# A decoder layer: scores on 32 rows of the array, all four self banks at once, biases added after the products

## What is computed

```
x = x + attention(layernorm(x))          # 16 heads of 32, rotary embedding, causal mask, biases on q, k, v, o
x = x + cross(layernorm(x), ctx)         # q = qdq(x) @ qdq(wq).T + bq ; k, v = ctx @ wkv.T + bkv
                                         # softmax without mask ; out = qdq(o) @ qdq(wp).T + bp
x = x + experts(layernorm(x))            # router softmax over 64 experts, top 8, at most 128 tokens an expert,
                                         # silu(x @ w_gate) * (x @ w_up) @ w_down, weighted sum
```

## Time and profile before

| | |
|---|---|
| three runs without profile | 1936.24, 1941.37, 1945.35 us, median 1941.37 |
| span of the profiled execution | 1982.1 us |
| PE busy | 1741.5 us (88%), 9128 instructions |
| PE weight loads | 1208.5 us (61%) |
| DVE busy | 1257.8 us (63%) |
| ACT busy | 928.6 us (47%) |
| POOL busy | 547.6 us (28%) |

### The profile page before, as it was taken

One profiled execution on the slowest core, in us unless ns is written; L12 is line 12 of the kernel. 1 busy time (PEld: TensorE's weight loads), 2 busy tenths in 40 slices (PEclk: granted clock), 3 DMA queues, 4 the chain that ended last, 5 costly groups with the idle time before them and its releaser, 6 DMA issues.

```text
span 1982.1 us, 31956 instructions
## 1 busy us (share of the span) xinstructions
PE 1741.5 (88%) x9128; PEld 1208.5 (61%) x9128; DVE 1257.8 (63%) x3136; ACT 928.6 (47%) x2737; POOL 547.6 (28%) x564
## 2 busy tenths in 40 slices
PE   3999999999999999999999999999957778778774
PEld 2676666666666666666666666666634455445453
DVE  7677777777777777777777777777743333333332
ACT  3465544555555445555554455555523333332331
POOL 4023223223332232223322322233222221212122
PEclk8999999999999999999999999999968988988887
DMA  9712121111101000000010000000075999998883
GB/s 355 254 45 95 72 81 73 68 60 57 41 25 38 27 21 21 21 21 21 21 34 24 26 21 21 21 21 21 22 197 157 233 237 224 230 229 219 226 216 43
DMA packets 119232, 190.29 MB, mean 96 GB/s; under 512 B 34373, under 2 KB 51141, under 8 KB 119208
## 3 DMA queue, kind: packets, MB, share of 16 engines
q1 hardware_dynamic: 89512, 154.20, 24.5%
q0 software_dynamic: 29696, 35.80, 9.4%
HBM read 126.61 MB, written 119.96 MB: 124 GB/s over the span
## 4 chain that ended last, share of the span: by engine, by line
PE 54%; DMA 22%; DVE 10%; issue 6%; ACT 5%; another core or an unknown queue 2%; POOL 0%; POOLq 0%; SPq 0%; DVEq 0%; ACTq 0%
PE bank L402 28%; DMA out<-x,slots 20%; PE bank L413 7%; PE bank L422 4%; PE bank L408 3%; PE bank L385 3%; ACT probs L678 3%; PE bank L430 3%; DVE kbd L1000 2%; PE bank L438 2%; DVE small L894 1%; PE bank L565 1%; DVE probs L1060 1%; PE bank L390 1%
## 5 line engine op out<-in xcount | busy, mean ns | idle before, releaser
L1224 POOL DMA_INDIRECT routed<-row,slots x256 | 268.2, 1047 | 284.9 <-DVE chosen_before L929 211.4
L678 ACT ACTIVATE probs<-bank,small 128x128 f32<-128x128 f32 x1024 | 322.3, 422 | 47.9 <-DVE small L894 47.2
L1216 POOL TENSOR_TENSOR small<-small,half 128x1 f32<-128x1 f32 x96 | 53.9, 562 | 628.3 <-DVE small L849 628.3
L894 DVE TENSOR_REDUCE small<-bank 128x4 f32<-128x512 f32 x256 | 171.2, 689 | 65.2 <-PE bank L416 47.1
L1304 POOL DMA_INDIRECT out<-x,slots x64 | 99.3, 1552 | 380.6 <-DVE slots L1176 265.4
L678 ACT ACTIVATION_READ_ACCUMULATOR probs<-bank,small 128x1 f32 x512 | 152.2, 301 | 0.0
L422 PEld LDWEIGHTS bank<-idf,probs 128*128 128x128 f32 x1024 | 119.2, 141 | 51.0 <-issue 28.0
L413 PE MATMUL bank<-kbd,qT 128*128 128x512 f32 x256 | 135.9, 612 | 6.7 <-DVE kbd L1000 6.7
L665 ACT ACTIVATE probsT<-bank 128x512 f32<-128x512 f32 x256 | 137.5, 636 | 6.1 <-PE bank L422 3.1
L422 PE MATMUL bank<-idf,probs 128*128 128x128 f32 x1024 | 138.3, 273 | 2.0 <-DVE probs L1060 1.4
L430 PEld LDWEIGHTS bank<-xv,probsT 128*128 128x128 f32 x1024 | 122.7, 193 | 11.1 <-issue 10.3
(11 more groups left out here) (249 smaller groups left out, 3982.4 us busy)
## 6 DMA issues: line engine op xcount, KB each, us to landing
w_gate_up<-in_w_gate SPq DMA_DIRECT2D x64, 384.0 KB
w_gate_up<-in_w_up SPq DMA_DIRECT2D x64, 384.0 KB
w_down<-in_w_down SPq DMA_DIRECT2D x64, 384.0 KB
routed<-empty_row SPq DMA_DIRECT2D x4, 4616.0 KB, 21.5
x_in<-in_x SPq DMA_DIRECT2D x32, 256.0 KB, 2.8
ctx_sb<-in_ctxT_in SPq DMA_DIRECT2D x32, 256.0 KB, 2.8
x_res<-in_x SPq DMA_DIRECT2D x32, 256.0 KB, 2.7
out<-x SPq DMA_DIRECT2D x32, 256.0 KB, 2.0
```

The lines of the kernel that those rows point to most:

```text
L678: last = act.activation(probs[:, g, j * P:(j + 1) * P], bank[:, b, j * P:(j + 1) * P], ACT.Exp, bias=negmax[:, h:h + 1], **({"accum_out": ...
L894: dve.tensor_reduce(negmax[:, g * GH:(g + 1) * GH], bank[:, b, :].rearrange("p (j k) -> p j k", j=GH), AX_X, ALU.max, negate=True).then_in ...
L1224: pool.indirect_dma_start(routed, bass.IndirectOffsetOnAxis(ap=slots[:, k:k + 1], axis=0), row[:, :], None, bounds_check=SLOTS - 1, oob_is ...
```

## The change

Three things at once.

*Scores on 32 rows.* The block-diagonal tiles go. `kT` and `xkT` hold the keys turned, heads of a group on 32 partitions each, and a head's scores are one product of 32 rows by 128 columns. A bank now holds the four heads that share a row group `j` (heads `j`, `j + 4`, `j + 8`, `j + 12`), and the sixteen products go round the four row groups and banks. So all four banks end together. `weigh`, `weigh_turned` and `average` follow the new order of heads, and the rows of Wo and the bias of v are permuted on the host.

*The four self banks at once.* All self scores are issued behind value products 1, with the four mask products ahead of them. Self scores 0 to 3 no longer stand between turns, value products and the turn of xk.

*No bias products.* The biases of q and k are rotated and turned once, and added in the copies to `qT` and `kT`; that of xk in the copy to `xkT`, now on DVE ahead of `norm_probs` 2; that of xv by POOL on `xv1` after the scatter; those of v and o become one table `att_bias` (an extra output projection before the loop), which POOL adds to `x_res` ahead of the scatter.

```diff
-            def project(b, hi, lo, name, first=0, end=1 + 3 * KT):
+            def project(b, hi, lo, name, first=0, end=3 * KT):
...
-                steps = [(bias_of[:, BIASES.index(name), :], bias_rows[:, :])]
+                steps = []
...
-            def scores(b, g, q, kb, causal_mask, done):
-
-                last = pe.matmul(bank[:, b, :], q[:, g, :], kb[:, g, :, :].rearrange("p j t -> p (j t)"),
-                                 start=True, stop=not causal_mask)
+            def scores(banks, rows_of, q, keys, causal_mask, done):
+
                 if causal_mask:
-                    last = pe.matmul(bank[:, b, :], idb[:, :], mask_add[:, :].unsqueeze(1).to_broadcast([P, GH, P]),
-                                     start=False, stop=True)
-                last.then_inc(done, 1)
+                    for b in banks:
+                        pe.matmul(bank[:, b, :], idb[:, :], mask_add[:, :].unsqueeze(1).to_broadcast([P, GH, P]),
+                                  start=True, stop=False)
+                for i in range(NG):
+                    for b, j in zip(banks, rows_of):
+                        own = slice(j * DH, (j + 1) * DH)
+                        last = pe.matmul(bank[:, b, i * P:(i + 1) * P], q[own, i, :], keys[own, i, :],
+                                         start=not causal_mask, stop=not causal_mask or i == NG - 1)
+                        if i == NG - 1:
+                            last.then_inc(done, 1)
...
-                    for g in range(NG):
-                        scores(CROSS_BANK[g], g, cqT, xkbd, False, p_xs)
+                    scores(CROSS_BANK, range(GH), cqT, xkT, False, p_xs)
                 for g in range(NG):
                     if with_cross:
                         until(pe, a_xexp, nth(prev, 4, g + 1))
                         turn_probs(CROSS_BANK[g], g, p_xpT)
-                    if with_self and g < 2:
-                        if g == 0:
-                            until(pe, d_qT, cur)
-                            until(pe, a_kbd, cur)
-                            until(pe, d_kbd, cur)
-                        scores(SELF_BANK[g], g, qT, kbd, True, p_s)
                 if with_self:
                     until(pe, a_xk, cur)
+                if with_cross:
+                    until(pe, g_xvb, prev)
                 for g in range(NG):
                     if with_cross:
                         until(pe, a_xpT, nth(prev, 4, g + 1))
                         weigh(5 if g < 2 else 7, g, xv1, p_xpv)
-                    if g == 0 and with_self:
-                        scores(0, 2, qT, kbd, True, p_s)
+                    if g == 1 and with_self:
+                        until(pe, d_qT, cur)
+                        until(pe, d_kT, cur)
+                        scores(SELF_BANK, range(GH), qT, kT, True, p_s)
                 if with_self:
                     turn(1, xk_sb, p_xkT)
-                    scores(4, 3, qT, kbd, True, p_s)
                     project(3, cT_hi, cT_lo, "xv").then_inc(p_xv, 1)
...
+                project(4, attT_hi, attT_lo, "o").then_inc(s_wT, 1)
...
-                if with_self:
-                    until(act, p_qkT, nth(cur, 2, 2))
-                    until(act, p_s, nth(prev, 4, 4))
-                    spread_keys(6, kbd, (0, 1)).then_inc(a_kbd, 1)
...
-                        if g == 3:
-                            until(act, p_xkT, cur)
-                            until(act, p_xs, nth(prev, 4, 4))
-                            spread_keys(1, xkbd, range(GH)).then_inc(a_xkbd, 1)
...
-                    until(dve, s_x_res, prev * 16)
+                    until(dve, g_res, prev)
...
-                    dve.tensor_scalar(qT[:, :, :].rearrange("p g t -> p (g t)"), bank[:, 2, :], SCALE, None,
-                                      ALU.mult).then_inc(d_qT, 1)
+                    dve.scalar_tensor_tensor(out=qT[:, :, :].rearrange("p g t -> p (g t)"), in0=bank[:, 2, :],
+                                             scalar=SCALE, in1=q_biasT[:, :], op0=ALU.mult,
+                                             op1=ALU.add).then_inc(d_qT, 1)
...
-                    for j in (2, 3):
-                        last = dve.tensor_copy(kbd[j * DH:(j + 1) * DH, :, j, :],
-                                               bank[j * DH:(j + 1) * DH, 6, :].rearrange("p (g t) -> p g t", g=NG))
-                    last.then_inc(d_kbd, 1)
+                    dve.tensor_tensor(wide_a[:, 0:D], bank[:, 6, :], k_biasT[:, :], ALU.add).then_inc(d_kT, 1)
...
+                if with_self:
+                    until(dve, p_xkT, cur)
+                    dve.tensor_tensor(xkT, bank[:, 1, :].rearrange("p (g t) -> p g t", g=NG),
+                                      xk_bias[:, :].unsqueeze(2).to_broadcast([P, NG, P]), ALU.add).then_inc(d_xkT, 1)
                 if with_self:
                     norm_probs(2, cur)
                     norm_probs(3, cur)
...
+                if with_self:
+                    if not with_cross:
+                        pool.wait_ge(s_wprep, 7)
+                    until(pool, s_x_res, cur * 16)
+                    pool.tensor_tensor(x_res[:, :], x_res[:, :], att_bias[:, :], ALU.add).then_inc(g_res, 1)
                 if with_before:
                     scatter(prev - 1)
+                if with_self:
+                    until(pool, a_xv, cur)
+                    pool.tensor_tensor(xv1[:, :, 0:DH], xv1[:, :, 0:DH],
+                                       xv_bias[:, :].rearrange("p (h d) -> p h d", h=H), ALU.add).then_inc(g_xvb, 1)
...
-            for n, kb in enumerate((kbd, xkbd)):
-                pool.wait_ge(s_wprep, n + 2)
-                pool.memset(kb[:, :, :, :], 0.0).then_inc(s_zeroed, 1)
```

More of the change, by code:

```diff
@@ L141, in layer @@
         qT = sb("qT", [P, NG, P])
-        kbd = sb("kbd", [P, NG, GH, P])
+        wide_a = sb("wide_a", [P, 4 * D])
+        kT = wide_a[:, 0:D].rearrange("p (g t) -> p g t", g=NG)
         v_sb = sb("v_sb", [P, D])
@@ L153, in layer @@
         xk_sb = sb("xk_sb", [P, D])
-        xkbd = sb("xkbd", [P, NG, GH, P])
+        wide_b = sb("wide_b", [P, 4 * D])
+        xkT = wide_b[:, 0:D].rearrange("p (g t) -> p g t", g=NG)
         xv1 = sb("xv1", [P, H, VW])
@@ L232, in layer @@
         g_x1b, g_tok = sem("pool_x1_bias"), sem("pool_token_number")
+        g_res, g_xvb = sem("pool_residual_bias"), sem("pool_xv_bias")
         weights_in = (("q", qT_w), ("k", kT_w), ("v", vT_w), ("xk", xkT_w), ("xv", xvT_w), ("o", oT_w))
         BY_DVE = 4
-        STAGE = [probs, probsT] + [t[:, :, :, :].rearrange("p g j t -> p g (j t)") for t in (kbd, xkbd)]
-        N_CONST = 12
+        STAGE = [probs, probsT] + [t[:, :].rearrange("p (g n) -> p g n", g=KT) for t in (wide_a, wide_b)]
+        N_CONST = 15
         W = {}
@@ L249, in layer @@
             w_dn.append(sb(f"w_down{k}", [FP, 2, D]))
-        tiles = [t[:, :, :, :].rearrange("p g j t -> p (g j t)") for t in (kbd, xkbd)] + \
+        tiles = [t[:, :] for t in (wide_a, wide_b)] + \
                 [t[:, :, :].rearrange("p g n -> p (g n)") for t in (probs, probsT)]
@@ L425, in weigh @@
             def weigh(b, g, vals, done):
-                for j in range(GH):
-                    h = g * GH + j
-                    at = (h % 8) * VW
-                    last = pe.matmul(bank[:, b, at:at + VW], probsT[:, g, j * P:(j + 1) * P], vals[:, h, :],
+                for i in range(NG):
+                    h = i * GH + g
+                    at = (g % 2 * NG + i) * VW
+                    last = pe.matmul(bank[:, b, at:at + VW], probsT[:, g, i * P:(i + 1) * P], vals[:, h, :],
                                      start=True, stop=True)
@@ L434, in weigh_turned @@
             def weigh_turned(b, g):
-                for j in range(GH):
-                    h = g * GH + j
-                    last = pe.matmul(bank[j * DH:(j + 1) * DH, b, g * P:(g + 1) * P], v_sb[:, h * DH:(h + 1) * DH],
-                                     probsT[:, g, j * P:(j + 1) * P], start=True, stop=True)
+                for i in range(NG):
+                    h = i * GH + g
+                    last = pe.matmul(bank[i * DH:(i + 1) * DH, b, g * P:(g + 1) * P], v_sb[:, h * DH:(h + 1) * DH],
+                                     probsT[:, g, i * P:(i + 1) * P], start=True, stop=True)
                 last.then_inc(p_pv, 1)
@@ L665, in copy @@
                 act.activation(dst, src, ACT.Copy).then_inc(done, 1)
-            def spread_keys(b, kb, heads):
-                for j in heads:
-                    last = act.activation(kb[j * DH:(j + 1) * DH, :, j, :],
-                                          bank[j * DH:(j + 1) * DH, b, :].rearrange("p (g t) -> p g t", g=NG), ACT.Copy)
-                return last
             def exponentials(b, g, done, total=None):
@@ L1120, in _ @@
             dve.wait_ge(s_const, 16 * N_CONST)
[L1121 to L1126 removed]
+            for src, at, crossed in ((x1, 0, xk_sb), (x2, D, xn2)):
```

(11 more changed lines are left out.)

107 lines of the change are left out of this document (54 added, 53 removed).

## The result

The change makes the kernel slower. In one comparison the kernel after took 1983.76 us (median of 1978.12, 1982.40, 1985.11 and 1990.07), the kernel before 1940.84 (median of four, 1936.24 to 1945.35): a ratio of 1.0231, 95% interval 1.0205 to 1.0257, +42.9 us. I had forecast slower with 0.71 and +88 us.

The account below looks back on a forecast made before the run. PE was taken as the loop's limit, with DVE not far behind. A period going from 42.5 to 45.1 us over 31 periods gave +81, plus +7 before the loop: 2029 us from 1941, range 1905 to 2105.

Parts of the forecast that it names:

- period before, no lateness: Attention loop of the kernel before: 43.85 us in the profile less 1.3 recorder cost, 42.5 without profile.
- period after, clock held: Attention loop after the change with TensorE at the same clock: 42.4 us a period, against 42.5 before.
- price of the clock: Loop: clock falls at 17 to 20 us each period until xv, +2.7 us; as a rival 1990 to 2065, chance 0.46.
- before the loop: Ahead of the loop: bias tables turned and added on DVE, extra output projection on PE; +7 us, bounds +3 and +10.
- the timetable: One loop period step by step: self chain starts 2.6 us later, PE's saving turns into waiting, next x1 at 42.4.
- What the change saves on PE: Loop period: bias products 3.7, cross scores 2.3, self scores 2.3, together 8.3 us of 42.6 busy.
- Rival 4: Score products: row groups don't run side by side, 2.6 us more per score group, 2106 us; chance 0.14.
- rival 5: Loop: clock falls a second time, from 33 to 37.5 behind the wait for xo8, 1.9 us more, 2088; chance 0.08.
- The lag: Loop: PE's completions 2 to 3 us behind its records, taken as the recorder's own cost, 1.3 us a period.
- Rival 3: Loop: lag is the chip's, not the recorder's; late completions get taken up afterwards, -38 us, 1903; chance 0.15.
- The side case of rival 2: Clock holds, but POOL's sum on xv1 delays DVE's last normalisation, +1.0 us a period, 1976; within a chance of 0.17.

Follow-up runs that it names:

- e5: Kernel before with one of the eight scatters of a body instead of eight: 1925.08 us, 0.9673 of the kernel before with eight.
- e7: Kernel after with one scatter of eight and filler products under the cross exponentials and behind xv: 1914.44 us, 0.9605 of the kernel before with eight.
- e6: Kernel after with one scatter of the eight: 1967.56 us, 0.9887 of the kernel before with eight.
- e8: Kernel after, one scatter, fillers under cross exponentials only, self groups 0 and 1 behind the turn of cross group 0, 2 and 3 behind value products 1: 1869.61 us.
- e11: e10 with self groups 2 and 3 issued ahead of the value products instead of behind value products 1: 1905.14 us, 0.9822 of the kernel before.
- e10: Kernel after with all eight scatters, order and fillers of e8 and the pauses between scatters of e9: 1913.57 us, 0.9882 of the kernel before.
- e0: Kernel before, unchanged, profiled a second time: 2016.34 us against 2014.44, ratio 1.0009.
- e1: Kernel after with idle stretches of TensorE filled by bf16 products whose results nobody reads: 2030.03 us, 1.0069 of the kernel before.
- e9: Kernel after with eight scatters, GpSimd writing a 128x512 tile that nobody reads between each two: 1999.77 us, 1.0341 of the kernel before.

## Why the prediction came out as it did

| term | forecast | measured |
|---|---|---|
| period before, no lateness | 42.5 | 42.36 (e5) |
| period after, clock held | 42.4 | 41.87 (e7) |
| price of the clock | +2.7 | +1.64 (e6 less e7) |
| before the loop | +7 | +4.3 (83.7 - 79.4, eight scatters), +2.7 (82.4 - 79.7, e6 less e5) |

Together 31 x (41.87 - 42.36 + 1.64) + 4.3 = +40 us, against +42.9. Taken with the profile of the kernel after itself, 31 x (43.62 - 42.36) + 4.3 = +43.4. Of the 45 us between forecast and result the clock makes 33 (31 x 1.06), the timetable 16 (31 x 0.53) and the part before the loop 3; the period before was 4 the other way. That adds up to 48, so 3 us are left over.

**What the change saves on PE: right in its parts.** 1.17 us for sixteen products on four row groups, 1.1 forecast; `project` starts with a plain product. The sum of 8.3 us is not measured as such: PE's busy time in a period goes from 42.6 to 36.5, with 3.4 us at the low clock in the latter. Rival 4, row groups one by one, is refuted by the same row.

**The timetable: right, and the core of the result.** All that is saved on PE gives 0.5 us of period with the clock held (42.36 to 41.87), because the self scores stand behind the cross exponentials and copies. That they set the period, e8 shows against e7, and e11 against e10, where nothing but their place is changed.

**The clock: the mechanism right, the size wrong.** The term that was mis-sized is "I expect a fall at about 17 to 20 in each period, and a return only in the dense `xv` projection": 2.7 a period. It falls there in 17 of 29 periods, in 12 of them it is back within 3.4 us, at a price of at most 0.6, and only in five it stays low to 27, for 3.3 us. The other place is rival 5's, 33 to 37, in 16 of 29 periods at 1.5 us. The Trainium skill (TensorE: Matmul & The Clock Gate, Part 4) says that turns don't keep the clock up as products do; the trace agrees as far as the fall at 17 us comes when PE has only turned or stood idle since the scores. It doesn't tell turns from idle time, and neither does e7, whose products fill the idle time too; e11 has a fall without idle time, but under value products.

**The lag: wrong.** "I take the lag as the recorder's own cost." Two profiles agreed with their runs (e0 2015 among 2008 to 2023, the kernel after 1978.12 among 1978 to 1990). The lateness is in PE's increments while the scatters are issued, and only in some sittings. That the median of 1941 was free of it is inferred: e5 takes 1925 with a period of 42.36, and 12 us of what it saves lie behind the loop (530.6 us from the last `x1` to the end, 543.2 in the first profile), which makes 1937 for eight scatters without lateness. So 42.5 was the right number for a wrong reason, and the forecast of 2070 for the profile missed by 92 us.

**Rival 3: half right.** The lag is in the execution, not in the recording. But I had let it hurt only the kernel before. In the one sitting with lateness in which both kernels ran the change costs 10%, since it moves the increments on which DVE waits under the scatters. I never asked what else ran at 22 to 31 us.

**The side case of rival 2 did not come.** POOL's sum on `xv1` starts 0.12 us after DVE's normalisation at 644.77, which keeps its 0.69 in this and all other periods. POOL pays:

```profile
644.89 1.62 POOL L1271 TENSOR_TENSOR xv<-xv,xv_bias 128x512 f32<-128x512 f32 x1 [4.44 <-ACT xv L679]
```

In e11 the same sum takes 1.18 to 1.22 where no such DVE instruction runs beside it. `cT_lo`, the like form, takes 1.29. There POOL starts first, and DVE's small instruction waits. I had charged DVE without asking who starts first; here the second is POOL, and it has slack. The Trainium skill (SBUF — State Buffer, Who interferes with whom) says that whoever issues first keeps the shared port; both pairs of rows agree.

**Before the loop: near the lower bound**, 4.3 or 2.7 of +3 to +10.

## What to carry to other kernels

Work taken off the busiest engine is worth only what the chain of first results lets through: put the shortened work where its consumers are already waiting, or the gain becomes idle time, and a thinner stretch of work may cost clock. When a profile and the runs disagree, take a second profile before giving the difference a cause. And a gap that the profile puts down to "remote", behind an engine that had long finished, is a wait in its own right: look at what else is being issued then, and don't move what others wait for under it.

## What the runs showed of the hardware that I had not expected

- TensorE's increments can reach the other engines 3 us (kernel before, once 4.5) or 5 us (e1) behind its recorded ends while GpSimd issues eight indirect DMAs 1.28 us apart; with one they never did, nor where the second or third of the eight came so late that only three were issued. In some sittings they are on time with eight. DVE's increments to ACT were on time meanwhile. What carries them, and what differs between sittings, no run here shows. Beside it the same kernel took 1937 or 1989 us on one chip, and the kernel after 1984 or 2199.
- A fall of the clock to 1.2 GHz costs 0.1 to 0.6, 1.5, 2.0 or 3.3 us a period by where it lies and how long it lasts, and in e11 it came behind 10.7 us in which PE was hardly idle; 26 small products a period, whose results nobody reads, took 53 us off a 1968 us kernel (e6 to e7).
- A DVE instruction of 128x512 with one input took 1.18 instead of 0.43 us beside GpSimd's memset of a tile of that size, and 0.43 to 0.61 beside a scatter alone (e9, e10).
